# Attention steps in another order: the small product ahead of the pairs, the values behind them, and VectorE's chains cut into pieces

## The reference

```
x  = group_norm(image) + pos                       # then group_norm again: sh
w  = sigmoid(conv1x1(silu(conv3x3(silu(conv1x1(x))))))     # 16 channels inside
a  = softmax attention of sh, 8 heads of 16        # "convolution stage"
m  = 2 heads of 64: queries from x*w, keys from sh
y  = group_norm(out(ff2(silu(ff1([a, m]))))) + image
t  = y + softmax attention of layer_norm(y), 8 heads of 16    # "token stage"
t  = t + sum over the top 2 of 8 experts: gate * w2(gelu(w1(layer_norm(t))))
```

## Time and profile before

| what | value |
| --- | --- |
| median of 3 runs | 3233.34 us (3230.92 to 3241.52) |
| the profiled execution | 3235.03 us, span of its instructions 3233.2 us |
| TensorE matmuls busy | 2605.7 us (81%) |
| VectorE busy | 2092.0 us (65%) |
| ScalarE busy | 1686.7 us (52%) |
| GpSimd busy | 625.0 us (19%) |
| mean granted clock of TensorE | 0.924 of full speed |
| row maxima (L1400) | 1152 reductions, 1365.8 us busy, 1220 ns each |
| exponentials of the two stages (L1205) | 1024, 1011.9 us busy, 1022 ns each |

### The profile page before, as it was taken

The page is one execution under the profiler, slowest core; times in us unless marked ns, Lnnn a source line. Parts: engine busy times, 40 slices in busy tenths (PEclk is TensorE's granted clock), DMA queues, the critical chain, the costliest instruction groups (busy, mean ns, idle before and its releaser), DMA issues. The chain is left out here.

```text
span 3233.2 us, 40732 instructions
## 1 busy us (share of the span) xinstructions
PE 2605.7 (81%) x14912; PEld 1000.2 (31%) x14912; DVE 2092.0 (65%) x3215; ACT 1686.7 (52%) x2470; POOL 625.0 (19%) x539
## 2 busy tenths in 40 slices
PE   4685787987889787897889878897878978898745
PEld 1122122352225322262222622244222522226125
DVE  3766677576775767667685667757676576756620
ACT  1452465555555465555654555554655546545623
POOL 4000022024110240103310141102311024010222
PEclk9997798999899898998999989999999989899967
DMA  4002210273004530153201730036301443016224
GB/s 108 2 1 46 56 25 14 79 185 65 6 20 139 122 66 2 53 178 68 48 10 57 206 68 8 14 119 148 66 1 53 148 79 67 5 50 191 37 75 145
DMA packets 155196, 228.88 MB, mean 71 GB/s; under 512 B 24368, under 2 KB 72432, under 8 KB 154912
## 3 DMA queue, kind: packets, MB, share of 16 engines
q1 hardware_dynamic: 146848, 209.78, 25.5%
q0 software_dynamic: 8192, 16.79, 2.0%
HBM read 174.29 MB, written 52.20 MB: 70 GB/s over the span
## 5 line engine op out<-in xcount | busy, mean ns | idle before, releaser
L1400 DVE TENSOR_REDUCE blockmax<-ps 128x2 f32<-128x1024 f32 x1152 | 1365.8, 1220 | 530.4 <-PE ps L764 426.8
L1205 ACT ACTIVATE prob<-ps 128x1024 f32<-128x1024 f32 x1024 | 1011.9, 1022 | 634.2 <-PE ps L942 631.3
L942 PE MATMUL ps<-qs,ks 99*128 99x512 bf16 x2048 | 633.1, 413 | 305.8 <-DVE blockmax L1400 168.5
L942 PEld LDWEIGHTS ps<-qs,ks 99*128 99x128 bf16 x2048 | 159.6, 102 | 683.8 <-DVE blockmax L1400 347.6
L600 POOL TENSOR_TENSOR rs<-vn,vec 128x1 f32<-128x1 f32 (+1 forms) x40 | 40.1, 1002 | 1350.3 <-DVE vn L1343 970.8
L959 PE MATMUL ps<-prob,va_a 128*32 128x512 f32 x2048 | 300.0, 660 | 0.0
L959 PE MATMUL ps<-prob,va_b 128*32 128x512 f32 x2048 | 297.4, 655 | 0.7 <-ACT prob L1205 0.7
L1252 ACT ACTIVATE prob<-ps,b1t 128x128 f32<-128x128 f32 x736 | 209.8, 369 | 162.9 <-PE ps L1039 162.8
L1230 ACT ACTIVATE prob<-ps 128x1024 f32<-128x1024 f32 x128 | 130.1, 1023 | 160.0 <-PE ps L996 92.4
L643 POOL DMA_INDIRECT x_dram<-ta,slot_u x128 | 124.3, 971 | 418.6 <-DVE slot_u L1623 382.0
L611 POOL DMA_INDIRECT routed<-y_dram,slot_u x128 | 122.3, 955 | 363.8 <-DMA y_dram<-prob 327.9
(11 more groups left out here) (238 smaller groups left out, 3184.4 us busy)
## 6 DMA issues: line engine op xcount, KB each, us to landing
parts_dram<-parts SPq DMA_DIRECT2D x32, 768.0 KB, 3.8
ks<-parts_dram SPq DMA_DIRECT2D x192, 128.0 KB, 4.9
qs<-parts_dram SPq DMA_DIRECT2D x192, 128.0 KB, 6.9
shared<-in_w SPq DMA_DIRECT2D x96, 256.0 KB, 3.3
prob<-in_w SPq DMA_DIRECT2D x96, 256.0 KB, 3.3
routed<-in_w SPq DMA_DIRECT2D x80, 256.0 KB, 3.5
xe<-in_w SPq DMA_DIRECT2D x48, 256.0 KB, 3.3
oatt<-in_w SPq DMA_DIRECT2D x48, 256.0 KB, 3.1
```

The source lines that it names most:

```text
L942: mm = pe.matmul(slot_banks(n + pr)[:, j, :], ks[:, slot_of(a, g), h, t * P:(t + 1) * P], qs[:, slot_of(a, g), h, cols(q)], start=True, st ...
L1205: act.activation(prob[:, n % 3, 2 * pr:2 * pr + 2, :], slot_banks(n + pr), ACT.Exp, scale=HD ** -0.5).then_inc(exp_done[a], 1)
L1400: dve.tensor_reduce(cells, banks, AX.X, ALU.max).then_inc(blocks_used[f], 1)
```

## The change

In a step of either stage TensorE now takes the first and the second scores, then the small products of this step, then the two pairs, and last the values of the step before. The values of a token stage's last step move into step 0 of the next pass (`weigh_last_values`), and ScalarE's copy of that output behind the exponentials of that step. VectorE takes in a step first the small products, then the two reductions, then the extras; `stream`, `look_ahead` and `reduce_next` are gone. The long chains are cut in pieces in the tables (`stats_e0`, `stats_e1`, `aggr_e`, `norm_e0`, `norm_e1`, `find0`, `find1`, `slots_k`, `slots_e`, `start_x0`, `start_x2`), and many entries of the tables get other steps; step 18 of the convolution stage now has two small products. The second convolution is one product: each quarter of the image goes to its own group of 32 output partitions, so ScalarE and VectorE read 128x256 in place of twice 16x512; the third convolution reads it quarter by quarter. Its weights and bias are loaded four times at the start. On GpSimd, `pre_rstd` stands ahead of the gathers, and `norm_rstd` among them.

```diff
-CONV_WINDOW = {1: ["tro0"], 2: ["tro1"], 3: ["tro2"], 4: ["tro3"], 5: ["turn_a1_1"], 8: ["tra0"], 9: ["trn0"],
-               10: ["trn1"], 11: ["km0"], 12: ["logits"], 13: ["turn_a1_2"], 14: ["km1"], 15: ["qm0"], 16: ["qm1"],
-               17: ["slots"], 20: ["tra1"], 21: ["turn_a1_3"], 23: ["trg0"], 24: ["trg1"], 25: ["b20"], 26: ["b21"],
-               27: ["tra2"], 29: ["turn_a1_4"]}
-CONV_EXTRA = {4: ["stats_e"], 6: ["norm_e"], 14: ["routes"], 20: ["gates"], 30: ["biases"]}
+CONV_WINDOW = {1: ["tro0"], 2: ["tro1"], 3: ["tro2"], 4: ["tro3"], 5: ["turn_a1_1"], 9: ["tra0"], 11: ["trn0"],
+               12: ["trn1"], 13: ["turn_a1_2"], 14: ["logits"], 15: ["km0"], 16: ["km1"], 17: ["qm0"],
+               18: ["qm1", "slots"], 20: ["tra1"], 21: ["turn_a1_3"], 23: ["trg0"], 24: ["trg1"], 25: ["b20"],
+               26: ["b21"], 27: ["tra2"], 29: ["turn_a1_4"]}
+CONV_EXTRA = {6: ["stats_e0"], 7: ["stats_e1"], 8: ["aggr_e"], 9: ["norm_e0"], 10: ["norm_e1"], 15: ["find0"],
+              16: ["find1"], 17: ["routes"], 19: ["slots_k"], 20: ["slots_e"], 22: ["gates"], 30: ["biases"]}
...
-TOKEN_WINDOW = {3: ["pre"], 5: ["turn_b_1"], 7: ["norm"], 9: ["kA0"], 10: ["kA1"], 11: ["qA0"], 12: ["qA1"],
+TOKEN_WINDOW = {1: ["pre"], 5: ["turn_b_1"], 6: ["norm"], 9: ["kA0"], 10: ["kA1"], 11: ["qA0"], 12: ["qA1"],
                 13: ["turn_b_2"], 14: ["vA0"], 15: ["vA1"], 16: ["c10"], 17: ["c11"], 18: ["vm0"], 19: ["vm1"],
-                20: ["res0"], 21: ["turn_b_3"], 22: ["res1"], 23: ["c20"], 24: ["c21"], 26: ["c30"], 28: ["c31"],
+                20: ["res0"], 21: ["turn_b_3"], 22: ["res1"], 24: ["c2"], 26: ["c30"], 28: ["c31"],
                 29: ["turn_a0_0"]}
-TOKEN_EXTRA = {1: ["start_pre"], 4: ["start_x1"], 8: ["start_xh"]}
+TOKEN_EXTRA = {0: ["start_pre"], 2: ["start_x0"], 3: ["start_x1"], 4: ["start_x2"], 7: ["start_xh"]}
...
+                for q in range(4):
+                    sp.dma_start(sa3w[quarter(q), :], sa3[0:HD, :]).then_inc(weights_in, 16)
+                    sp.dma_start(vec_b2[quarter(q), :], vecs[0:HD, :]).then_inc(weights_in, 16)
...
                         if token and front and (k, t) == (1, NT // 2):
-                            rstd("pre_rstd", 1)
+                            rstd("norm_rstd", 1)
...
                 keep_parts_b()
+                if experts and front:
+                    rstd("pre_rstd", 1)
                 if experts:
                     gather_rows()
...
+                elif name == "c2":
                     pe.wait_ge(done["conv_in"], 6)
                     for dy in range(3):
-                        mm = pe.matmul(ps[0:HD, SM, :], sa2w[:, dy, :],
-                                       conv_in[:, 16 * h + dy:16 * h + dy + 16, :].rearrange("p y x -> p (y x)"),
-                                       start=(dy == 0), stop=(dy == 2))
+                        for q in range(4):
+                            mm = pe.matmul(ps[quarter(q), SM, 0:2 * P], sa2w[:, dy, :],
+                                           conv_in[:, 8 * q + dy:8 * q + dy + 8, :].rearrange("p y x -> p (y x)"),
+                                           start=(dy == 0), stop=(dy == 2))
...
+            def weigh_last_values():
+
+                t, n = NT - 1, 2 * STEPS - 1
+                for j in range(GH):
+                    c = VW * (2 * j + 1)
+                    mm = pe.matmul(ps[32 * j:32 * j + 32, OB, :], va[1][:, t, c:c + 2 * HD], prob[:, n % 3, j, :],
+                                   start=False, stop=True)
+                mm.then_inc(last_weighed, 1)
+
+            def attention_step(a, n, pairs, run, names):
 
                 if run:
                     scores(a, n, 0)
                     scores(a, n, 1)
+                if a == 0 and n == 0 and experts:
+                    weigh_last_values()
+                for name in names:
+                    small_product(name)
+                for i, (f, d) in enumerate(pairs):
+                    max_pair(a, n, i, f, d, run)
                 if run and n:
                     weigh_values(a, n - 1)
-                for i, (f, d) in enumerate(pairs):
-                    max_pair(a, n, i, f, d, run)
...
             def link(ins):
 
                 note(ins)
-                reduce_next()
                 sync()
...
-            def attention_step(n, names, extra):
-
-
-                step[0] = last[0] = n
-                while stream and stream[0][0] <= n:
-                    reduce_next()
+            def attention_step(n, pairs, names, extra):
+
                 for name in names:
                     small_product(name)
-                    last[0] = n
+                for i, (f, d) in enumerate(pairs):
+                    reduce_pair(f, d, slot_banks(n + 2 + i))
                 for name in extra:
                     small_product(name)
-                    last[0] = n
```

More of the change, by code:

```diff
@@ L230, in build @@
         low = sb("low", [96, S])
-        conv2, gate_t = low, low[0:NE, :]
+        gate_t = low[0:NE, :]
         parts = sb("parts", [P, 2, 3, S], BF16)
@@ L356, in cols, with quarter @@
             return slice(h * HALF, (h + 1) * HALF)
+        def quarter(q, rows=HD):
+            return slice(32 * q, 32 * q + rows)
+        conv2 = tb[:, 0:2 * P]
         def two(ap):
@@ L660, in pool_program @@
                     rstd("pre_rstd", 1)
-                rstd("norm_rstd", 1)
+                    rstd("norm_rstd", 1)
                 for i, x in enumerate("kq"):
@@ L1082, in tensor_program @@
                 for n in range(2 * STEPS):
-                    attention_step(1, n, token_pairs(n, token, front), token)
-                    for name in small.token.get(n, ()):
-                        small_product(name)
-                if token:
-                    weigh_values(1, 2 * STEPS - 1)
+                    attention_step(1, n, token_pairs(n, token, front), token, small.token.get(n, ()))
         def scalar_program(act, conv, experts, token, front, small):
@@ L1215, in scalar_program @@
                         exps(0, n)
+                    if n == 0 and experts:
+                        act.wait_ge(last_weighed, 1)
+                        act.activation(oatt[:, 3, :], ps[:, OB, :], ACT.Copy).then_inc(last_taken, 1)
                     for name in small.conv.get(n, ()):
                         small_product(name)
-                    if n == 17 and experts:
+                    if n == 18 and experts:
                         act.wait_ge(done["gate_diff"], 1)
@@ L1288, in vector_program @@
             chain = [0]
-            stream = []
-            step, last = [0], [0]
             def note(ins):
@@ L1298, in sync @@
                 dve.wait_ge(dve_chain, chain[0])
-            def reduce_next():
-                if stream and stream[0][0] <= last[0]:
-                    reduce_pair(*stream.pop(0)[1])
-            def look_ahead(steps):
-                last[0] = step[0] + steps
             def link(ins):
                 note(ins)
-                reduce_next()
                 sync()
@@ L1318, in freed, with group_stats @@
             def freed(name):
-                reduce_next()
                 dve.wait_ge(small_free, small[name])
-            def group_stats(src, name, before=""):
-                for h in range(2):
+            def group_stats(src, name, before="", start=0):
+                for h in range(start, 2):
                     if before:
@@ L1338, in group_var @@
                 freed(name)
-                look_ahead(steps)
                 link(dve.tensor_tensor(nb[:, 0:1], gs[:, 0:1], gs[:, 0:1], ALU.mult))
@@ L1349, in group_coefs, with token_stats @@
                 link(dve.tensor_tensor(cb[:, :], v(f"{name}_b"), nb[:, 0:1], ALU.subtract))
-            def layer_stats(src, name, before=""):
-                for t in range(NT):
+            def token_stats(src, tiles, before=""):
+                for t in tiles:
                     if before and t % 4 == 0:
@@ L1552, in small_product @@
                 elif name == "tr_x":
-                    layer_stats(tok, "b", "tok")
-                    layer_norm(tok, "b")
+                    token_stats(tok, range(NT), "tok")
+                    token_var("b")
+                    token_norm(tok, "b", range(NT))
                 elif name in ("ff2", "tr_nb"):
@@ L1578, in small_product, with find_choices @@
                                           ).then_inc(done["k_even"], 1)
+            def find_choices(h):
+                sync()
+                for t in range(4 * h, 4 * h + 4):
+                    note(dve.max_index(topi[:, t, :], top[:, t, :], logit[:, t, :]))
+                if h == 0:
+                    return
+                sync()
+                link(dve.tensor_copy(topf[:, :, :], topi[:, :, 0:2]))
+                dve.tensor_tensor(logit[:, :, :], logit[:, :, :], top[:, :, 0:1].to_broadcast([P, NT, NE]),
+                                  ALU.subtract).then_inc(done["gate_diff"], 1)
             def routes():
```

(10 more changed lines are left out.)

139 lines of the change are left out of this document (63 added, 76 removed).

## The result

The changed kernel takes 3193.5 us (median of four runs, 3190.8 to 3198.6), the kernel before beside it 3237.4: ratio 0.9867, 95% interval 0.9842 to 0.9892. It is faster, by 44 us or 1.3%; 110 had been forecast. The profiled execution took 3190.82 us (span 3189.0) against 3235.03.

A forecast was written before the change was run, and what follows sets the result against it. No engine is full: a loop of waits bounds the kernel. Six full images gain 87 us; with image 0, the last image and the first block, about 110 of 3235.0: 3125 us, own range 3095 to 3160, 8 in 10 within 3075 to 3215.

The forecast's parts named there:

- Plain step 3.11: Step without VectorE small work: scores, exponential, second pair, values close a loop of 3.11 us, 0.14 less than now.
- turn: Step where VectorE waits for the closed unit and splits its maxima in 1.2 us: 4.15, against 3.45 now.
- Token steps 1 to 16: Token stage, image 1: step 16's scores start at 774.35 instead of 779.89, after a 1.1 us wait.
- `c2` at 1.5: Second convolution's product as twelve 256-column matmuls in four column groups: 1.5 us; 5.3 without overlap.
- First block: Convolution's two products at the low clock gain 6 us; eight added loads ahead of VectorE's constants cost 5.5.
- The step that failed: Token stage, steps 17 to 31: 50 us instead of 54.3, summed from prices per step.
- its sign of being wrong: Prediction wrong if the convolution stage grows beyond 118 us or the token stage shrinks by less than 5.
- I expect no fall of the clock: Token step 16: its wait is 1.1 us in place of 4.4, so no clock fall; first reduction at 776.7, not 783.9.
- clock: Rival, chance 0.14: new 4 to 6.6 us steps bring stretches at clock 0.5, 70 us in all: 3195.
- Chains in full: Rival, chance 0.10: VectorE's chains add to every step and plain steps stay at 3.25: about 3290 us.
- stalls stay: Rival, chance 0.06: row DMAs land as late as now, only plain steps gain: 3205 to 3220 us.
- more hidden: Rival, chance 0.15: plain steps at 2.85, single chains in the bubble, shorter `k`/`q` steps: 3085 likely, 3045 far end.

The follow-up runs named there:

- both repairs: Changed kernel with the split's remainder kept in PSUM and ScalarE's copy of the output behind the small reads: 3131.3 us, ratio 0.9672.

## Why the prediction was wrong

- *Plain step 3.11*: right (3.10 between scores, 2.85 while catching up), and so was nearly every step of the convolution: `tro` 3.58 for 3.72, turn 4.22 for 4.15, step 18 6.79 for 6.6; the two at the logits, 5.82 and 4.38 for 4.8 and 3.2, were over. With its boundary the stage gained some 4 us per image, 3 forecast.
- *Token steps 1 to 16*: right to 0.2 us at step 16's scores, in part by luck. The chain of 13.4 us is there, but the 1.1 us that TensorE was to stand at its end are not: the turn of step 12 to 13, held up by GpSimd, took 5.12 in image 1 where 4.15 were forecast, and used them up. The error named below was here too, and cost little here.
- *`c2` at 1.5*: the product took 1.49.
- *First block*: it gave 4.2, 0.5 forecast. The two products that the prediction put at the low clock take 5.28 and 5.30 in the trace of the kernel before, but its granted clock reads 1.00 there; why they are slow stays open.
- **The step that failed**: "Steps 17 to 31 are now 54.3. After: `c11` 3.25, ... turn 4.15, ... `c2` 4.8, ... turn 4.15, ...: 50.5, or 48 where the turns are made up; 50." It took 59.0 in image 1, and the stage shrank by 2.3, under the 5 that the prediction had named as its sign of being wrong. These chains were priced on VectorE and TensorE alone. ScalarE's reads had been followed for `trn0`, `k` and `q`, but not here: the output's copy waits for the values, and the reads of `c10` and `c2` stand behind it (1.1 and 2.2 us, shown by moving the copy). And the split was priced with the 1.2 us of a chain that GpSimd does not hold up: 0.7, 1.2 and 1.6 us in three turns (shown by keeping the remainder in PSUM). Together 6.9 of the 11.0 us per image that the repairs give back.
- *"I expect no fall of the clock"* was said of step 16 and silently carried over to the rest. The other 4.1 us are steps with unchanged instructions; the time at 0.5 per middle image falls from 32 to 17 us with both repairs, and the six stages after, drawn against their time at 0.5 (20 to 48 us), rise by 0.34 us for each us: 5. Step 25 to 26 alone is 1.3 of the 4.1, and goes with the clock as shown above. That the clock is the whole of those 4.1 was not tried by itself.
- The *clock* rival named 3195, the time that came, but for another reason: most of the loss is in the two waits, and the token stages' time at 0.5 falls from 224 to 121 us when they go. *Chains in full*, *stalls stay* and *more hidden* did not come.

The wait behind GpSimd could have been read beforehand. The kernel before has it in its trace, at the turn of step 29 of all seven token stages with a next front (timeline, image 1; the shortest cast there takes 0.21):

```profile
832.39 2.13 POOL L702 TENSOR_TENSOR parts<-parts,mrow 128x1024 bf16<-128x1024 bf16 x1
...
834.01 0.58 DVE L1418 CAST maxrow<-rowrem 16x128 bf16<-16x128 f32 x1
```

The Trainium skill (SBUF — State Buffer, "SBUF: two separate sides") says that VectorE and GpSimd share one pair of ports, which is locked for a whole instruction, and that VectorE needs it in a 2-port mode or, against a GpSimd instruction that reads SBUF, with two SBUF inputs. The trace of the changed kernel agrees: the cast from SBUF 2.04 and the subtraction with two SBUF sources 1.19 beside GpSimd, 0.28 each with a PSUM source. Both the row and the rule spoke against putting the split in front of the reductions; the prediction did not weigh it.

## What to carry to other kernels

When an instruction moves, list everything that waits for it on every engine, and what stands in order behind those waits: here the values moved on TensorE, and the cost came up in ScalarE's queue and VectorE's. A chain put on the path has to be priced beside the engine that shares its port, and a buffer that is shared in order (a DMA queue, a small bank) moves a wait further on when the first one is cured. In these runs the clock also fell behind steps that stood long, and the steps behind them took longer with the same instructions; count that with it.

## What was not expected of the hardware

- A row store and load on SP's queue takes 1.4 us from store to load with nothing ahead, 5.1 behind six spreads, 10.1 behind eighteen.
- VectorE reading PSUM with an SBUF operand beside a running GpSimd instruction is not held up at all (34 of 34 at 0.28).
- Stages with the same instructions differ with their time at 1.2 GHz (0.5), though not in proportion: the convolution stages took 839, 846 and 847 us in sum in three kernels that share them, with 89, 119 and 111 us at 0.5.
- A fall to 0.5 need not follow a TensorE that stands: of the 68 stretches in the kernel before, three (at 1275.1, 1654.0 and 2415.2) begin behind the logits' small matmuls and four scores, while the trace shows TensorE's matmuls following each other without a gap.
